# Paged attention: the keys of a page ordered by their number modulo four, so that the weight loads of the probability transpositions read packed columns

## The reference, cut to what matters

```python
kc = k_cache[block_table].reshape(bsz, L, HK, D)      # L = 16 pages x 32 keys, HK = 8, D = 128
k_all = jnp.concatenate([kc, k], axis=1)              # 512 cached + 32 new keys
valid_c = jnp.arange(L)[None, :] < cache_seqlens[:, None]
scores = jnp.einsum('bqhd,bkhd->bhqk', q, k_all) * SCALE
scores = jnp.where(valid[:, None, None, :], scores, -1e+30)
probs = jax.nn.softmax(scores, axis=-1)
o = jnp.einsum('bhqk,bkhd->bqhd', probs, v_all)
```

## Time and profile before

| | us |
|---|---|
| median of 3 runs | 3421.36 (3420.88 to 3421.98) |
| profiled execution: its span | 3419.6 |
| attention, from the first score to the last value product | about 1627 to 2895 of the span |
| TensorE busy in the span | 3310.5 (97%) |
| VectorE busy | 2328.7 (68%) |
| ScalarE busy | 1764.8 (52%) |
| GpSimd busy | 1323.4 (39%) |

### The profile page before, as it was taken

The page is one execution under the profiler, slowest core; times in us unless marked ns, Lnnn a source line. Parts: engine busy times, 40 slices in busy tenths (PEclk is TensorE's granted clock), DMA queues, the critical chain, the costliest instruction groups (busy, mean ns, idle before and its releaser), DMA issues. The chain is left out here.

```text
span 3419.6 us, 69875 instructions
## 1 busy us (share of the span) xinstructions
PE 3310.5 (97%) x22398; PEld 3056.2 (89%) x22398; DVE 2328.7 (68%) x6644; ACT 1764.8 (52%) x4307; POOL 1323.4 (39%) x2391
## 2 busy tenths in 40 slices
PE   7799999999899999999999999999999999999999
PEld 5688899988778888888999999999999998888878
DVE  6445544445577778878898888888888886423274
ACT  4323222233237888878566666666666665422222
POOL 0231100000017887887555555555555553100002
PEclk9899999999999999999999999999999999999999
DMA  5413422334645555556766666656666665533353
GB/s 205 138 57 73 122 81 80 85 121 138 203 142 185 171 175 180 180 176 211 237 214 208 214 217 216 211 185 211 211 214 213 216 218 192 174 107 111 114 180 104
DMA packets 448054, 571.96 MB, mean 167 GB/s; under 512 B 171657, under 2 KB 330185, under 8 KB 430794
## 3 DMA queue, kind: packets, MB, share of 16 engines
q1 hardware_dynamic: 427978, 429.08, 39.7%
q0 software_dynamic: 19712, 138.42, 11.5%
HBM read 394.60 MB, written 172.75 MB: 166 GB/s over the span
## 5 line engine op out<-in xcount | busy, mean ns | idle before, releaser
L2622 PE MATMUL l2a_x<-l2a_pt,l2a_V 128*128 128x128 f32 x4096 | 542.9, 276 | 1.0 <-DVE l2a_pn L2556 1.0
L2622 PEld LDWEIGHTS l2a_x<-l2a_pt,l2a_V 128*128 128x128 f32 x4096 | 504.0, 193 | 1.1 <-issue 1.1
L2534 DVE CUSTOM_DVE_ANT_0 l2a_sm<-l2a_s,l2a_B 128x544 f32<-128x544 f32 x512 | 369.6, 722 | 92.6 <-PE l2a_s L197 79.7
L2489 ACT ACTIVATE l2a_p<-l2a_sm,l2a_st 128x544 f32<-128x544 f32 x512 | 380.0, 742 | 26.8 <-DVE l2a_st L2537 26.5
L2344 POOL CAST l2a_K<-cache 128x256 fp32r x768 | 294.6, 435 | 221.7 <-issue 221.7
L2344 POOL CAST keys<-cache 128x256 fp32r x750 | 299.3, 451 | 192.9 <-issue 137.4
L2475 ACT ACTIVATE l2a_pt<-l2a_t 128x512 f32<-128x512 f32 x512 | 305.7, 597 | 127.6 <-PE l2a_t L2605 126.3
L2605 PE MATMUL l2a_t<-ident,l2a_p 128*128 128x128 f32 x2048 | 334.3, 286 | 5.4 <-ACT l2a_ao L2482 5.4
L2547 DVE TENSOR_SCALAR l2a_p<-l2a_p,l2a_st 128x512 f32<-128x512 f32 x512 | 282.0, 551 | 18.2
L2605 PEld LDWEIGHTS l2a_t<-ident,l2a_p 128*128 128x128 f32 x2048 | 287.7, 209 | 6.5 <-issue 5.9
L2482 ACT ACTIVATE l2a_ao<-l2a_x 128x128 f32<-128x128 f32 x512 | 142.2, 278 | 281.9 <-PE l2a_x L2623 281.9
(11 more groups left out here) (856 smaller groups left out, 8667.0 us busy)
## 6 DMA issues: line engine op xcount, KB each, us to landing
s_qT<-l2q_qo SPq DMA_DIRECT2D x128, 512.0 KB
head<-s_qT SPq DMA_DIRECT2D x64, 512.0 KB
l2a_Q<-s_qT SPq DMA_DIRECT2D x64, 512.0 KB
s_ao<-l2a_ao SPq DMA_DIRECT2D x64, 512.0 KB, 4.9
l2o_a<-s_ao SPq DMA_DIRECT2D x128, 256.0 KB, 3.0
s_kn<-l2q_ko SPq DMA_DIRECT2D x128, 128.0 KB, 2.9
head<-s_kn SPq DMA_DIRECT2D x32, 512.0 KB, 5.8
wqraw<-in_wqkv SPq DMA_DIRECT2D x32, 384.0 KB, 3.8
```

The source lines that it names most:

```text
L2489: act.activation(prr[sc % 6][:, :], smr[sc % 2][:, :], ACT.Exp, bias=s[:, 1:2], scale=SCALE, accum_out=s[:, 2:3]).then_inc(exped, 1)
L2534: dve.tensor_tensor_reduce(out=smr[sc % 2][:, :], in0=ps_s[sc % 2][:, 224:768], in1=Br[g % 2][:, :], scale=1.0, scalar=-3e38, op0=ALU.add, ...
L2622: pe.matmul(px[:, P:256], V[:, k * D + hg * P:k * D + hg * P + P], pt[:, k, :], start=k == 0, stop=False)
```

## The change

The keys in a page (of the cache, as the host lays it out) stand by their number modulo four: position 8k+j holds key 4j+k. A score product takes two of the four classes over all 17 pages (272 columns, 8 adjacent columns at a time), so that the scores, and with them the probabilities, stand by class: 136 columns for each, 128 of the cached keys and 8 of the new ones. A transposition then reads 128 adjacent columns. The multiplication by the reciprocal takes 4 runs of 128 and 4 runs of 8. The mask's key numbers come in the new order from another constant. The new keys themselves and all value tiles stay as they are. The number and the sequence of instructions on each engine are the same; the six matmuls of a unit's scores are now all 272 columns wide instead of three of 288 and three of 256.

```diff
-            sp.dma_start(iota[:, :], A["iota544"]).then_inc(iota_in, 16)
+            sp.dma_start(iota[:, :], A["keypos"]).then_inc(iota_in, 16)
...
-                    dve.tensor_tensor_reduce(out=smr[sc % 2][:, :], in0=ps_s[sc % 2][:, 224:768], in1=Br[g % 2][:, :], scale=1.0,
+                    dve.tensor_tensor_reduce(out=smr[sc % 2][:, :], in0=ps_s[sc % 2][:, 240:784], in1=Br[g % 2][:, :], scale=1.0,
...
-                    dve.tensor_scalar(p[:, 0:512], p[:, 0:512], s[:, 3:4], None, ALU.mult).then_inc(scaled, 1)
+                    p4 = p[:, :].rearrange("p (k n) -> p k n", k=4)
+                    dve.tensor_scalar(p4[:, :, 0:P], p4[:, :, 0:P], s[:, 3:4], None, ALU.mult).then_inc(scaled, 1)
...
-                    dve.tensor_scalar(pNr[g % 3][:, 32 * hg:32 * hg + 32], p[:, 512:544], s[:, 3:4], None, ALU.mult).then_inc(newed, 1)
+                    dve.tensor_scalar(pNr[g % 3][:, 32 * hg:32 * hg + 32].rearrange("p (k j) -> p k j", k=4), p4[:, :, P:136],
+                                      s[:, 3:4], None, ALU.mult).then_inc(newed, 1)
...
-                    for o, pg in ((224, slice(0, 9)), (512, slice(9, 17))):
-                        m = mm3(pe, s[:, o:o + 32 * (pg.stop - pg.start)],
-                                [((Q[:, hg, 0, :], Q[:, hg, 1, :]), (K[:, pg, 0, c], K[:, pg, 1, c]))])
+                    for o, c in ((240, 32 * hg), (512, 32 * hg + 16)):
+                        keys = [K[:, :, z, c:c + 16].rearrange("p g (k j) -> p k g j", k=2) for z in range(2)]
+                        m = mm3(pe, s[:, o:o + 272], [((Q[:, hg, 0, :], Q[:, hg, 1, :]), keys)])
...
-                        m = pe.transpose(ps_t[tr % 2][:, k, :], p[:, k:512:4], ident[:, :])
+                        m = pe.transpose(ps_t[tr % 2][:, k, :], p[:, 136 * k:136 * k + P], ident[:, :])
...
+    by_rest = lambda a: a.reshape(a.shape[:-1] + (8, 4)).swapaxes(-1, -2)
+    keypos = by_rest(iota.reshape(17, 32)).swapaxes(0, 1).reshape(544)
...
-        "kT": c(inputs["L2_cond_k_cache"].transpose(0, 3, 2, 1).reshape(64, P, 2, P).transpose(2, 0, 1, 3)),
+        "kT": c(by_rest(inputs["L2_cond_k_cache"].transpose(0, 3, 2, 1)).reshape(64, P, 2, P).transpose(2, 0, 1, 3)),
```

More of the change, by code:

```diff
@@ L2580, in _ @@
                     Q, K, s = Qr[g], Kr[g % 2], ps_s[sc % 2]
-                    c = slice(32 * hg, 32 * hg + 32)
                     if sc in fill:
@@ L3010 @@
         "invf": c(np.broadcast_to(invf, (P, 64))), "iota544": c(np.broadcast_to(iota, (P, 544))),
+        "keypos": c(np.broadcast_to(keypos, (P, 544))),
         "qnorm": c(inputs["L2_cond_q_norm_w"]), "knorm": c(inputs["L2_cond_k_norm_w"]),
```

## The result

| | median us (runs) | ratio to before, 95% interval |
|---|---|---|
| before | 3421.12 (4) | |
| changed | 3444.64 (3438.68 to 3447.99, 4) | 1.0068 [1.0056, 1.0081] |

What follows compares the result with a forecast made beforehand. TensorE was taken as the bound in attention. From the profiled span, 3419.6 - 25.2 (transpositions) + 0 (scores, VectorE) = 3394.4 us, with 1.8 us to the median 3396.2 us, 0.74% less; range 3393 to 3422 us.

Steps and rivals of the forecast that it cites:

- The bound: Middle of attention: TensorE busy 200.00 of 200 us, so a nanosecond off a unit's matmuls comes off 512 times.
- The transpositions: In attention, packed columns cut each from 122.3 to 110 ns start to start, saving 25.2 us over 2048.
- The second rival: Transpositions: the stride is not what makes them slow, or the load is hidden anyway; 3421.4 us, chance 0.06.
- The scores: Six score matmuls a unit: same columns, 153 more jumps between runs; cost taken as 0, up to 28 us.
- The upper end: Score matmuls: all 16 ns of excess blamed on 45 jumps, 0.36 ns each, so 153 more cost 28 us.
- the stage with contiguous operands: Stage ahead of attention: 3 ns excess a matmul without jumps, against 2.7 in the scores, so jumps are not to blame.
- The rule of the Trainium skill: SBUF reads: 16-byte lines need two hits for full bandwidth; runs of 8 have four, so scores cost nothing more, sum -25.2 us.
- The last rival: Score reads: a jump costs more than the bound, say 0.83 ns, 65 us in all, net 3461 us; chance 0.04.
- VectorE: Its large multiplication over 4 runs of 128 keeps two elements a cycle; cost taken as 0, 266 ns if lost.
- The third rival: VectorE's multiplication loses its double rate to the gaps, chain 2.51 us a unit, +59, 3480 us; chance 0.06.
- The gather of values: Attention's value loads land in 5.6 to 9.4 us; issue lead shrinks from 10.4 to 10.2 us, 0.8 us left.
- The announced test: Prediction wrong if scores' distance grows over 8 ns each, or TensorE has idle time in the middle of attention.

Runs made afterwards that it cites:

- Run 2: The kernel before with only its transpositions reading 128 adjacent columns each (values then meet wrong keys): 3392.92 us, ratio 0.9916 to before.
- run 5: The changed kernel with score matmuls reading 272 adjacent columns of the key tile, no jumps (other keys than wanted): 3391.6 us.
- run 6: The changed kernel with score matmuls reading 34 runs of 8 columns 64 bytes apart (other keys than wanted): 3388.6 us.
- run 7: The changed kernel with score matmuls reading 34 runs of 8 columns 512 bytes apart, in two dimensions (other keys than wanted): 3452.9 us.
- run 9: The changed kernel with its three-dimensional score pattern, but 992 bytes from page to page instead of 1024 (other keys than wanted): 3385.9 us.
- run 10: The changed kernel with score matmuls reading 34 runs of 8 columns 256 bytes apart (other keys than wanted): 3459.0 us.
- run 11: The changed kernel with score matmuls reading 34 runs of 8 columns 480 bytes apart (other keys than wanted): 3387.5 us.
- run 13: The changed kernel, right result, with 8 spare columns after each page in the odd sequences' key tile only: 3414.14 us, ratio 0.9982 to before.
- run 15: The changed kernel with score matmuls reading 34 runs of 8 columns 128 bytes apart (other keys than wanted): 3388.2 us.
- run 8: The kernel before, keys and scores unchanged, with ScalarE's exponential writing by class so transpositions read packed columns, right result: 3394.51 us, ratio 0.9927 to before.
- run 12: The changed kernel, right result, reading two classes of a page together (runs of 16) and sorting them in the matmul's output pattern: 3396.76 us, ratio 0.9943 to before.
- run 3: The changed kernel with score matmuls reading 16 adjacent columns of each of 17 pages, classes left mixed in the scores: 3395.3 us.

## Why the prediction was wrong, point by point

- **The bound.** Right: TensorE without a hole in the middle of attention, before and after, so that unit times carry through. The sum of the two group differences (-24.3 and +48.0) is +23.7, against +23.5 in the medians and +20.3 in the profiled spans; that it meets the medians within 0.3 us is luck.
- **The transpositions.** Right: 110 ns against 110.5 measured, 25.2 us against 24.3 by busy time and 23 by the distances. The group came out at 310 us and not 316, since a packed transposition's record lasts 274 ns in the mean and the sum kept the 286 of the strided ones. Run 2 shows the gain by itself. The second rival (the stride is not the cause) is out.
- **The scores: the step that failed.** "So the excess goes with a busy stage and not with jumps. I take 0 and keep 28 us for the range." The term of the sum was 0; the cost was 48.0 us, 93 ns a unit, beyond the end that was called a bound. Two mistakes are in it. The upper end was a price per jump from runs of 32 columns, 0.36 ns, carried over to runs of 8; against adjacent columns the price of a jump to the next page was 11 / 45 = 0.24 ns at 32 columns, 0.18 at 16, 0.53 at 8 and 0.39 at 4. It does not follow from the price at another length, so a row with long runs bounds nothing for short ones; and it is no price of jumps as such, since 198 jumps at 992 bytes cost nothing. And the stage with contiguous operands that has 3 ns of excess as well was taken to explain the excess of the scores; run 5 shows 757 ns without jumps, so that 11 of the 14 ns went with jumps.
- **The rule of the Trainium skill** (SBUF — State Buffer, "Door 1: The DMA port swizzle"), 16-byte lines and two hits on each, gave 0 for the scores. It fits the transpositions (121.8 ns with one hit a line, 109.1 packed) and the runs 64 bytes apart (752 ns). At 256, 512 and 1024 bytes from run to run there are four hits on every line as well, and the measured 884, 874 and 861 ns contradict it as a complete rule; the measurement decides.
- **The last rival** (a jump costs more than the bound; chance 0.04) is what happened, at 93 / 153 = 0.61 ns for each added jump, under the 0.83 used as its example and over the 0.41 from which it is a loss; but it is the step of 1024 bytes that makes them dear, which the rival did not name. "It needs short runs to be costlier than long ones" was the right condition, at that step, and got too small a chance: for an access that no row shows, the losing side deserved a share near that of the forecast.
- **VectorE.** Right: its multiplication over 4 runs of 128 has a median of 486 ns against 490; the double rate stays, and its mean fell from 551 to 524. The third rival is out.
- **The gather of values**: lands in 5.6 to 9.7 us against 5.6 to 9.4, and TensorE waits for none of it.
- **The announced test** ("if the scores' distance has grown by more than 8 ns each") is what the trace shows: 93 / 6 = 15.5 ns.

## What to carry to other kernels

Before the data of a bound engine are regrouped so that one operand is read packed, look at what the other operand turns into: write down length, number and step of its runs, and treat a pattern that no row of the trace shows as unknown, not as free. Steps of 256, 512 or 1024 bytes under runs of 32 bytes were slow here, and eight spare columns per page cured it in the tile that had them. Where an order has to be changed, let an engine with idle time write it (here ScalarE), or an output pattern that costs nothing (here the matmul's).

## What the runs showed of the hardware that was not expected

- A moving operand of 34 runs of 8 fp32 columns costs 752 to 764 ns for six matmuls of 272 columns at steps of 64, 128, 480, 992 and 1056 bytes, like adjacent columns (757), and 861 to 884 at 256, 512 and 1024 (runs 5 to 7, 9 to 11, 13 and 15, and the changed kernel). At 1024 bytes runs of 16 columns cost 774, runs of 4 cost 915. Whether other multiples of 256 bytes are slow, and in which part of the memory the reads meet, is not shown.
- A transposition whose weight load reads every fourth column of fp32 takes 121.8 ns to the next start, with adjacent columns 109.1 (run 2); the load's record is 209 ns long against 140 to 143 (run 8 and the changed kernel).
- The matmul's output in runs of 8 columns (32 bytes) in PSUM cost nothing: 774 ns in run 12, 774 in run 3.
- ScalarE's exponential over 544 columns took 743 ns with an adjacent output and 1267 ns with a step of 544 bytes between elements (run 8), 0.96 ns a column more.
